# Weight low parts on one engine and four normalisations moved from VectorE to ScalarE, in a one-core layer tower

## The chip, the core and the metric

The kernel runs on one core of a Trainium2 chip. The metric is the device time of one execution in microseconds (us), as the median of several runs. Engines are named as in the profile: PE (TensorE matmul), PEld (its weight loads), DVE (VectorE), ACT (ScalarE), POOL (GpSimd) and SP (SyncE, which issues most DMAs).

## What is computed

Eight sequences of 512 tokens go through an embedding, a linear-attention block with memory, and a mixture of 64 experts with two shared ones, all in fp32. Cut to what matters here:

```python
h = concat(fine_embed[ids], softmax(cluster_logits[ids]) @ coarse_embed)   # (8, 512, 128)
x = layernorm(h)                                       # x1 in the kernel
xn = rms_norm(x)                                       # xn: one scale and shift of h
x = x + mem_scale * (((xn@q)(xn@k)^T * decay) @ (xn@v)) @ o
xn2 = rms_norm(x)
y = x + op_scale * gelu(xn2 @ read @ mix + bias) @ write
h = h + y
x3 = layernorm(h)
gates = top6(softmax(x3 @ router + bias)), with a capacity per expert
out = h + shared_ffn(x3) / 2 + sum_e gates[e] * (silu(x3@gate[e]) * (x3@up[e])) @ down[e]
```

## The kernel before

The experts are taken two at a time, as 33 **pairs** of 128 hidden columns (pair 0 is the shared one). For each pair `gate_up` (L470) issues three fp32r matmuls of 128x512 for gate and three for up, because each fp32 operand is held as a high part and a low part (`gate_hi`, `gate_lo`, `x_hi`, `x_lo`; the products are hi*hi, lo*hi and hi*lo). ACT applies Silu (L603), DVE multiplies by up (L855), POOL multiplies by the row of gates (L1016), and `down` (L449) adds the product into `bank_y`; for odd pairs `hid` is split too, by ACT (L609) and DVE (L861).

Each engine has its own instruction queue, written out by hand in one order. `sequences` (L259) calls one function per engine for each sequence b; its loop runs over p = 0..32, and at the slots of the tables `PE_AT`, `ACT_AT`, `DVE_AT`, `POOL_AT` it slips in the steps of the next sequence (`*_late(b+1)`, attention and router) and of the one after (`*_early(b+2)`, embedding). So the attention of sequence b+1 hides under the experts of sequence b. Sequence 0 has nothing to hide under: its early and late steps run alone, in an **opening** of two such loops ahead of `sequences` (pairs 0 and 1 of its experts are put there at slot 30). Banks: pair p of gate and of up uses one of two PSUM banks each, so `gate_up(p)` waits for Silu and the up product of pair p-2. `down` runs four pairs behind.

In the opening the weights arrive too: gate and up in six chunks of 11 pairs (`CHUNKS`, 704 KB each, issued by SP at L330), each into a staging buffer that is also something else (`hid`, `gate_rows`, `later`). `split_hi` (ACT, L637) copies the chunk rounded to fp32r into the high part; `split_lo` (L271, on DVE or on POOL by the table `LO_AT`) subtracts it to get the low part, and frees the buffer. Four staging buffers serve six chunks, so the last two chunks wait for a low part. `down_hi` (ACT, L656) and `down_lo` (DVE, L951) do the same for the down weights of odd pairs.

The four normalisations of a sequence, each four instructions of 128x128 on DVE, are `xn` (L671, slot 0), `x1` (L677, slot 5), `xn2` (L720, slot 11) and `x3` (L743, slot 19); the inverse roots come from POOL (L986, L992, L997). For example:

```python
last = dve.tensor_scalar(xn[:, t, :], emb[par][:, t, :], mv1[:, t, 0:1], inv1[:, 1, t:t + 1],
                         ALU.subtract, ALU.mult)
```

## Time and profile before

| | us |
|---|---|
| median of 3 runs (lowest, highest) | 746.45 (746.19, 747.09) |
| the profiled execution, its own time | 748.99 |
| its span, first to last instruction | 746.8 |
| busy in the span: PE, PEld | 689.9, 516.6 |
| busy in the span: DVE, POOL, ACT | 526.0, 471.0, 350.4 |

Busy time is the sum over an engine's instructions. A matmul's end is modelled and matmuls are pipelined, so PE's busy share tells only whether it had something in flight; how fast it went is seen from the distance between the starts of two matmuls, or from the granted clock. An instruction that is long because it was held up counts as busy for its whole length.

### The profile page before, as it was taken

The page shows a single profiled execution, that of the slowest core. Times are in us where ns is not written, and L with a number is a line of the kernel's source. Part 1 is how long each engine was busy: PE and PEld are TensorE (multiplying, and loading weights), DVE is VectorE, ACT ScalarE, POOL GpSimd, SP SyncE. Part 2 cuts the span into 40 slices and gives each one's busy share as a digit, 9 for nine tenths or more (in the row PEclk, how much of TensorE's full clock was granted, in tenths as well). Part 3 has the DMA queues.
Part 4 walks back from the last instruction along what each step waited for, and adds up shares of the span by engine and source line. Part 5 has one row for each costly group of instructions (what it writes and reads, how often), then busy time and mean ns, then how long its engine had stood idle before and what let it go on. Part 6 is the DMA issues. An engine that isn't in the chain of part 4 may idle for free.

```text
span 746.8 us, 10995 instructions
## 1 busy us (share of the span) xinstructions
PE 689.9 (92%) x2943; PEld 516.6 (69%) x2943; DVE 526.0 (70%) x1070; ACT 350.4 (47%) x607; POOL 471.0 (63%) x352
## 2 busy tenths in 40 slices
PE   4355799999999999989999999999999999999997
PEld 3244577777777767757777777777777777777775
DVE  4846767798678877775777886698777866684443
ACT  3323355534744455523645446544645445543342
POOL 5511657667676757656666766667766656676664
PEclk8555899999999999989999999999999999999999
DMA  5500423333333423333333333334334434335431
GB/s 206 205 1 0 121 85 106 107 110 112 110 100 113 119 88 116 111 99 109 95 107 112 109 111 110 113 82 133 107 100 114 120 93 119 100 112 136 131 123 57
DMA packets 48868, 80.31 MB, mean 108 GB/s; under 512 B 9504, under 2 KB 13728, under 8 KB 48800
## 3 DMA queue, kind: packets, MB, share of 16 engines
q1 hardware_dynamic: 47776, 77.44, 33.9%
q0 software_dynamic: 1024, 2.10, 1.3%
q8 instruction: 27, 0.44, 0.2%
q14 instruction: 41, 0.34, 0.1%
HBM read 76.35 MB, written 3.15 MB: 106 GB/s over the span
## 4 chain that ended last, share of the span: by engine, by line
PE 89%; DVE 5%; issue 2%; ACT 1%; POOL 0%; DVEq 0%; POOLq 0%
PE bank_y L468 15%; PE bank_g L479 8%; PE bank_g L480 8%; PE bank_u L481 8%; PE bank_u L479 8%; PE bank_g L481 8%; PE bank_u L480 8%; PE bank_y L463 4%; PE bank_y L462 4%; PE bank_y L465 4%; PE bank_f L387 1%; PE bank_f L409 1%; PE bank_f L403 1%; PE bank_f L420 1%; PE bank_f L379 1%
## 5 line engine op out<-in xcount | busy, mean ns | idle before, releaser
L1016 POOL TENSOR_TENSOR hid<-hid,gate_rows 128x512 f32<-128x512 f32 x256 | 372.5, 1464 | 195.9 <-DVE hid L855 193.2
L603 ACT ACTIVATE hid<-bank_g 128x512 f32<-128x512 f32 x264 | 156.6, 599 | 279.0 <-PE bank_g L481 268.2
L855 DVE TENSOR_TENSOR hid<-hid,bank_u 128x512 f32<-128x512 f32 x264 | 178.7, 681 | 139.5 <-PE bank_u L481 79.4
L479 PE MATMUL bank_g<-x_hi,gate_hi 128*128 128x512 f32 x264 | 144.1, 546 | 3.7 <-issue 3.7
L468 PE MATMUL bank_y<-hid,w_down 128*128 128x512 f32 x272 | 138.9, 592 | 0.0
L861 DVE TENSOR_TENSOR hid_lo<-hid,hid_hi 128x512 fp32r<-128x512 f32 x128 | 109.5, 855 | 2.6 <-issue 2.2
L480 PE MATMUL bank_g<-x_hi,gate_lo 128*128 128x512 f32 x264 | 105.5, 400 | 0.0
L481 PE MATMUL bank_u<-x_lo,up_hi 128*128 128x512 f32 x264 | 105.4, 399 | 0.0
L479 PE MATMUL bank_u<-x_hi,up_hi 128*128 128x512 f32 x264 | 105.3, 399 | 0.0
L481 PE MATMUL bank_g<-x_lo,gate_hi 128*128 128x512 f32 x264 | 105.2, 399 | 0.0
L480 PE MATMUL bank_u<-x_hi,up_lo 128*128 128x512 f32 x264 | 104.9, 397 | 0.0
L609 ACT ACTIVATE hid_hi<-hid 128x512 fp32r<-128x512 f32 x128 | 80.2, 627 | 7.9 <-POOL hid L1016 7.2
L479 PEld LDWEIGHTS bank_g<-x_hi,gate_hi 128*128 128x128 f32 x264 | 50.7, 192 | 28.9 <-issue 22.6
L480 PEld LDWEIGHTS bank_g<-x_hi,gate_lo 128*128 128x128 f32 x264 | 50.9, 193 | 23.7 <-issue 19.0
L468 PEld LDWEIGHTS bank_y<-hid,w_down 128*128 128x128 f32 x272 | 51.3, 189 | 11.9
L479 PEld LDWEIGHTS bank_u<-x_hi,up_hi 128*128 128x128 f32 x264 | 50.5, 191 | 12.1
L481 PEld LDWEIGHTS bank_g<-x_lo,gate_hi 128*128 128x128 f32 x264 | 50.3, 191 | 12.0
L481 PEld LDWEIGHTS bank_u<-x_lo,up_hi 128*128 128x128 f32 x264 | 50.1, 190 | 12.1
L480 PEld LDWEIGHTS bank_u<-x_hi,up_lo 128*128 128x128 f32 x264 | 50.2, 190 | 11.8
L462 PE MATMUL bank_y<-hid_hi,down_hi 128*128 128x512 f32 x128 | 52.0, 406 | 0.0
L463 PE MATMUL bank_y<-hid_hi,down_lo 128*128 128x512 f32 x128 | 51.5, 402 | 0.0
L465 PE MATMUL bank_y<-hid_lo,down_hi 128*128 128x512 f32 x128 | 51.1, 399 | 0.0
(197 smaller groups left out, 842.7 us busy)
## 6 DMA issues: line engine op xcount, KB each, us to landing
gate_rows<-gates_dram SPq DMA_DIRECT2D x512, 128.0 KB
hid<-gate_t_dram SPq DMA_DIRECT2D x3, 704.0 KB, 7.3
w_down<-down_t_dram SPq DMA_DIRECT2D x3, 704.0 KB, 6.7
out_dram<-later SPq DMA_DIRECT2D x8, 256.0 KB, 2.9
gate_rows<-up_t_dram SPq DMA_DIRECT2D x2, 704.0 KB, 4.9
gates_dram<-gates_t SPq DMA_DIRECT2D x8, 128.0 KB, 2.3
later<-up_t_dram SPq DMA_DIRECT2D x1, 704.0 KB, 8.5
shared<-square_w_dram SPq DMA_DIRECT2D x1, 512.0 KB
```

What stands on the lines that cost most here:

```text
L462: pe.matmul(y, down_hi[:, j, :], hid_hi[:, k, :], start=False, stop=False)
L463: pe.matmul(y, down_lo[:, j, :], hid_hi[:, k, :], start=False, stop=False)
L465: pe.matmul(y, down_hi[:, j, :], hid_lo[:, k, :], start=False, stop=False).then_inc(sem("down_done"), 1)
L468: pe.matmul(y, w_down[:, p, :], hid[:, slot(par, p), :], start=(p == 0), stop=(p == PAIRS - 1)).then_inc(sem("down_done"), 1)
L479: pe.matmul(o, w_hi[name][:, p, :], x3_hi[par][:, :], start=True, stop=False)
L480: pe.matmul(o, w_lo[name][:, p, :], x3_hi[par][:, :], start=False, stop=False)
L481: pe.matmul(o, w_hi[name][:, p, :], x3_lo[par][:, :], start=False, stop=True).then_inc(sem("pe_" + name), 1)
L603: act.activation(hid[:, slot(par, p), :], bank_g[(p + par) % 2][:, :], ACT.Silu).then_inc(sem("silu"), 1)
L609: act.activation(hid_hi[:, (p // 2) % SPLIT_RING, :], hid[:, slot(par, p), :], ACT.Copy)\
L855: dve.tensor_tensor(hid[:, s, :], hid[:, s, :], bank_u[(p + par) % 2][:, :], ALU.mult)\
L861: dve.tensor_tensor(hid_lo[:, k, :], hid[:, slot(par, p), :], hid_hi[:, k, :].bitcast(F32), ALU.subtract)\
L1016: pool.tensor_tensor(hid[:, s, :], hid[:, s, :], gate_rows[:, row, :], ALU.mult)\
```

## The change

The table `CHUNKS` now says of each chunk its staging buffer, the slot of its high part (ACT) and the slot of its low part, all on DVE (slots from 33 on lie in sequence 0's experts). The last two chunks have staging buffers of their own, so no chunk waits for another. `down_hi` goes from slot 26 to 10 of the opening, `down_lo` from slot 28 of the opening to slot 1 of sequence 0. DVE computes only the small shifts `-mean * inv` (`shift1`, `shift3`), and ACT does the normalisations as `Identity(scale * in + bias)`, `xn2` as a `Copy` with scale: `xn` in slot 0, `x1` in slot 3, `xn2` in slot 11, `x3` in slot 19. PE waits for the low parts chunk by chunk.

```diff
...
 SPLITS = PAIRS // 2
-DOWN_HI_AT, DOWN_LO_AT = 26, 28
+DOWN_HI_AT, DOWN_LO_AT = 10, PAIRS + 1
...
 GATHER_AT = (1, 2, 3, 4)
-DVE_AT = dict(xn=0, xn_lo=2, x1=5, xn_dec=5, y_lo=4, scores=6, state=6, x2=8, result=10, logits=9, xn2=11, exp_sum=12,
-              h=15, bn1=16, h2=17, bn3=17, mv1=18, x3=19, x3_lo=21, router=24, prob=26, top=27, chosen=28, gates=29,
+DVE_AT = dict(shift1=0, xn_lo=2, xn_dec=5, y_lo=4, scores=6, state=6, x2=8, result=10, logits=9, exp_sum=12,
+              h=15, bn1=16, h2=17, bn3=17, mv1=18, shift3=19, x3_lo=21, router=24, prob=26, top=27, chosen=28, gates=29,
               taken=31)
...
              router=23, gates_t=30)
-ACT_AT = dict(xn_hi=2, y_hi=4, z=6, ffn_t=5, squares=9, squares2=10, cluster_exp=10, exp_t=12, xn2_t=13, vals=14,
+ACT_AT = dict(xn=0, x1=3, xn2=11, x3=19, xn_hi=2, y_hi=4, z=6, ffn_t=5, squares=9, squares2=10, cluster_exp=10, exp_t=12, xn2_t=13, vals=14,
               x3_hi=21, router_exp=24)
...
 CHUNK = 11
-CHUNKS = [(n, p0) for p0 in range(0, PAIRS, CHUNK) for n in ("gate", "up")]
-HI_AT = (-20, -20, -20, -20, 4, 5)
-LO_AT = (("pool", -10), ("vector", 0), ("pool", -10), ("vector", 0), ("pool", 0), ("vector", 6))
-RAW_PARTS = 4
+CHUNKS = (("gate", 0, "hid0", None, -20, 3),
+          ("up", 0, "rows", None, -20, 10),
+          ("gate", CHUNK, "hid1", None, 3, 14),
+          ("up", CHUNK, "later", None, 5, 14),
+          ("gate", 2 * CHUNK, "own0", None, 5, PAIRS + 6),
+          ("up", 2 * CHUNK, "own1", None, 7, PAIRS + 9))
+CHUNK_OF = {(n, p0): k for k, (n, p0, *_) in enumerate(CHUNKS)}
 SHIFT = 3
...
         inv1 = sb("inv1", [P, 2, TILES])
+        shift1 = sb("shift1", [P, 2, TILES])
+        shift3 = sb("shift3", [P, TILES])
         x1 = sb("x1", [P, TILES, D])
...
-        raw = [b.rearrange("p r s -> p (r s)")[:, 0:CHUNK * P].rearrange("p (c d) -> p c d", c=CHUNK)
-               for b in (hid[:, 0:RING // 2, :], gate_rows[:, :, :], hid[:, RING // 2:RING, :], later[:, :, :])]
+        def staging(b):
+            return b.rearrange("p r s -> p (r s)")[:, 0:CHUNK * P].rearrange("p (c d) -> p c d", c=CHUNK)
+        raw = {"hid0": staging(hid[:, 0:RING // 2, :]), "hid1": staging(hid[:, RING // 2:RING, :]),
+               "rows": staging(gate_rows[:, :, :]), "later": staging(later[:, :, :]),
+               "own0": sb("raw0", [P, CHUNK, P])[:, :, :], "own1": sb("raw1", [P, CHUNK, P])[:, :, :]}
         gates_dram = nc.dram_tensor("gates_dram", (BATCHES, EXPERTS, SEQ), F32, kind="Internal").ap()
...
-        def weights_split(eng, chunks):
+        def staging_free(eng, buffer):
-            for part in range(min(RAW_PARTS, chunks)):
-                eng.wait_ge(sem(f"split_lo{part}"), (chunks - 1 - part) // RAW_PARTS + 1)
+            for k, c in enumerate(CHUNKS):
+                if c[2] == buffer:
+                    eng.wait_ge(sem(f"split_lo{k}"), 1)
-        def split_lo(eng, name, at):
-            for k, (n, p0) in enumerate(CHUNKS):
-                if LO_AT[k] == (name, at):
-                    eng.wait_ge(sem("split_hi"), k + 1)
-                    eng.tensor_tensor(w_lo[n][:, p0:p0 + CHUNK, :], raw[k % RAW_PARTS],
+        def split_lo(dve, at):
+            for k, (n, p0, buffer, _, _, lo_at) in enumerate(CHUNKS):
+                if lo_at == at:
+                    dve.wait_ge(sem(f"split_hi{k}"), 1)
+                    dve.tensor_tensor(w_lo[n][:, p0:p0 + CHUNK, :], raw[buffer],
                                       w_hi[n][:, p0:p0 + CHUNK, :].bitcast(F32), ALU.subtract)\
-                       .then_inc(sem(f"split_lo{k % RAW_PARTS}"), 1)
+                       .then_inc(sem(f"split_lo{k}"), 1)
+            if at == DOWN_LO_AT:
+                dve.wait_ge(sem("down_hi"), 1)
+                dve.tensor_tensor(down_lo[:, :, :], odd_pairs(w_down), down_hi[:, :, :].bitcast(F32), ALU.subtract)\
+                   .then_inc(sem("down_lo"), 1)
...
                 if isinstance(b, int) and b == 0:
-                    weights_split(sp, len(CHUNKS))
+                    staging_free(sp, "rows")
             if r >= GATE_RING:
...
-            def weights(k):
-                n, p0 = CHUNKS[k]
-                part = k % RAW_PARTS
-                if k >= RAW_PARTS:
-                    sp.wait_ge(sem(f"split_lo{part}"), k // RAW_PARTS)
-                sp.dma_start(raw[part], sources[n][:, p0:p0 + CHUNK, :]).then_inc(sem(f"raw{part}"), 16)
             sp.wait_ge(sem("gathered0"), 16 * TILES)
-            for k in range(len(CHUNKS)):
-                weights(k)
+            for k, (n, p0, buffer, before, _, _) in enumerate(CHUNKS):
+                if before is not None:
+                    sp.wait_ge(sem(f"split_lo{before}"), 1)
+                sp.dma_start(raw[buffer], sources[n][:, p0:p0 + CHUNK, :]).then_inc(sem(f"raw{k}"), 16)
             for p0 in range(0, PAIRS, CHUNK):
...
             q = PAIRS * b + p
+            if isinstance(b, int) and b == 0 and p % CHUNK == 0:
+                for n in ("gate", "up"):
+                    pe.wait_ge(sem(f"split_lo{CHUNK_OF[n, p]}"), 1)
             ring = (p + par) % 2
...
                     pe.wait_ge(sem("x3_lo"), 1)
-                    weights_split(pe, 2 * PAIRS // CHUNK)
                     for k in range(AHEAD):
...
             f0, f1 = bank_f
+            for name, k, out in (("xn", 1, xn), ("x1", 0, x1)):
+                if p == ACT_AT[name]:
+                    act.wait_ge(sem("shift1"), b + 1)
+                    for t in range(TILES):
+                        last = act.activation(out[:, t, :], emb[par][:, t, :], ACT.Identity,
+                                              scale=inv1[:, k, t:t + 1], bias=shift1[:, k, t:t + 1])
+                    last.then_inc(sem(name), 1)
+            if p == ACT_AT["xn2"]:
+                act.wait_ge(sem("inv2"), b + 1)
+                act.wait_ge(sem("xn_dec"), b + 1)
+                for t in range(TILES):
+                    last = act.activation(xn2[:, t, :], x2[:, t, :], ACT.Copy, scale=inv2[:, t:t + 1])
+                last.then_inc(sem("xn2"), 1)
+            if p == ACT_AT["x3"]:
+                act.wait_ge(sem("shift3"), b + 1)
+                for t in range(TILES):
+                    last = act.activation(x3[:, t, :], h2[par][:, t, :], ACT.Identity,
+                                          scale=inv3[:, t:t + 1], bias=shift3[:, t:t + 1])
+                last.then_inc(sem("x3"), 1)
             if p == ACT_AT["xn_hi"]:
...
             act.wait_ge(sem("pe_gate"), q + 1)
-            if isinstance(b, int) and b == 0 and p == 0:
-                weights_split(act, len(CHUNKS))
+            if isinstance(b, int) and b == 0 and p in (0, RING // 2):
+                staging_free(act, "hid1" if p else "hid0")
             wait(act, "down_done", q - RING + 1)
...
                     act_early(act, b + 2, p)
+                if first:
+                    split_hi(act, PAIRS + p)
                 act_silu(act, b, par, p)
...
         def split_hi(act, at):
-            for k, (n, p0) in enumerate(CHUNKS):
-                if HI_AT[k] == at:
-                    part = k % RAW_PARTS
-                    act.wait_ge(sem(f"raw{part}"), 16 * (k // RAW_PARTS + 1))
-                    act.activation(w_hi[n][:, p0:p0 + CHUNK, :], raw[part], ACT.Copy).then_inc(sem("split_hi"), 1)
+            for k, (n, p0, buffer, _, hi_at, _) in enumerate(CHUNKS):
+                if hi_at == at:
+                    act.wait_ge(sem(f"raw{k}"), 16)
+                    act.activation(w_hi[n][:, p0:p0 + CHUNK, :], raw[buffer], ACT.Copy).then_inc(sem(f"split_hi{k}"), 1)
...
             f0, f1 = bank_f
-            if p == DVE_AT["xn"]:
+            if p == DVE_AT["shift1"]:
                 dve.wait_ge(sem("inv1"), b + 1)
-                for t in range(TILES):
-                    last = dve.tensor_scalar(xn[:, t, :], emb[par][:, t, :], mv1[:, t, 0:1], inv1[:, 1, t:t + 1],
-                                             ALU.subtract, ALU.mult)
-                last.then_inc(sem("xn"), 1)
-            if p == DVE_AT["x1"]:
-                for t in range(TILES):
-                    last = dve.tensor_scalar(x1[:, t, :], emb[par][:, t, :], mv1[:, t, 0:1], inv1[:, 0, t:t + 1],
-                                             ALU.subtract, ALU.mult)
-                last.then_inc(sem("x1"), 1)
+                dve.scalar_tensor_tensor(shift1[:, :, :], mv1[:, :, 0].unsqueeze(1).to_broadcast([P, 2, TILES]), -1.0,
+                                         inv1[:, :, :], ALU.mult, ALU.mult).then_inc(sem("shift1"), 1)
             if p == DVE_AT["xn_dec"]:
...
                    .then_inc(sem("x2"), 1)
-            if p == DVE_AT["xn2"]:
-                dve.wait_ge(sem("inv2"), b + 1)
-                for t in range(TILES):
-                    last = dve.tensor_scalar(xn2[:, t, :], x2[:, t, :], inv2[:, t:t + 1], None, ALU.mult)
-                last.then_inc(sem("xn2"), 1)
             if p == DVE_AT["h2"]:
...
                 dve.tensor_scalar(var3[:, :], mv3[:, :, 1], LN_EPS, None, ALU.add).then_inc(sem("var3"), 1)
-            if p == DVE_AT["x3"]:
+            if p == DVE_AT["shift3"]:
                 dve.wait_ge(sem("inv3"), b + 1)
-                for t in range(TILES):
-                    last = dve.tensor_scalar(x3[:, t, :], h2[par][:, t, :], mv3[:, t, 0:1], inv3[:, t:t + 1],
-                                             ALU.subtract, ALU.mult)
-                last.then_inc(sem("x3"), 1)
+                dve.scalar_tensor_tensor(shift3[:, :], mv3[:, :, 0], -1.0, inv3[:, :], ALU.mult, ALU.mult)\
+                   .then_inc(sem("shift3"), 1)
             if p == DVE_AT["x3_lo"]:
...
                     dve_early(dve, b + 2, par, p, use)
+                if first:
+                    split_lo(dve, PAIRS + p)
                 dve_up(dve, b, par, p)
...
                         .then_inc(sem("decays"), 1)
-                split_lo(dve, "vector", p - PAIRS)
             dve.wait_ge(sem("decays"), 3)
...
                 dve_early(dve, 1, 1, p - SHIFT, 1, bank_y)
-                split_lo(dve, "vector", p)
-                if p == DOWN_LO_AT:
-                    dve.wait_ge(sem("down_hi"), 1)
-                    dve.tensor_tensor(down_lo[:, :, :], odd_pairs(w_down), down_hi[:, :, :].bitcast(F32), ALU.subtract)\
-                       .then_inc(sem("down_lo"), 1)
+                split_lo(dve, p)
             sequences(dve, lambda *a: dve_sequence(dve, *a))
...
                 pool_early(pool, 0, p)
-                split_lo(pool, "pool", p - PAIRS)
             for p in range(PAIRS):
...
                 pool_early(pool, 1, p - SHIFT)
-                split_lo(pool, "pool", p)
             sequences(pool, lambda *a: pool_sequence(pool, *a))
...
```

ACT's queue in the opening, from the second high part on: before,

```order
L637 ACTIVATE up_hi<-gate_rows 128x1408
L637 ACTIVATE gate_hi<-hid 128x1408
L637 ACTIVATE up_hi<-later 128x1408
L560 ACTIVATE x_hi<-bank_f 128x512
L563 ACTIVATE vo_y_hi<-bank_f 128x512
L637 ACTIVATE gate_hi<-hid 128x1408
L637 ACTIVATE up_hi<-gate_rows 128x1408
L567 ACTIVATE z<-bank_f 128x256 x2
L573 ACTIVATE shared,ss<-shared 128x128 x4
L577 ACTIVATE xn_t<-bank_f 128x512
```

and with the change:

```order
L664 ACTIVATE up_hi<-gate_rows 128x1408
L570 ACTIVATE xn<-emb,shift,inv 128x128 x4
L587 ACTIVATE x_hi<-bank_f 128x512
L570 ACTIVATE x<-emb,shift,inv 128x128 x4
L664 ACTIVATE gate_hi<-hid 128x1408
L590 ACTIVATE vo_y_hi<-bank_f 128x512
L664 ACTIVATE up_hi<-later 128x1408
L664 ACTIVATE gate_hi<-raw 128x1408
L594 ACTIVATE z<-bank_f 128x256 x2
L664 ACTIVATE up_hi<-raw 128x1408
L600 ACTIVATE shared,ss<-shared 128x128 x4
L683 ACTIVATE down_hi<-w_down 128x2048
```

`x<-` is `x1`, `shared,ss` the squares for `xn2`. The normalisations stand between the high parts; `x1` and one high part now lie ahead of `vo_y_hi`.

ACT's queue where sequence 0's experts begin, before,

```order
L587 ACTIVATE turns<-turns 128x256
L656 ACTIVATE down_hi<-w_down 128x2048
L603 ACT_TABLE_LOAD
L603 ACTIVATE hid<-bank_g 128x512 x2
L560 ACTIVATE x_hi<-bank_f 128x512
```

and with the change:

```order
L614 ACTIVATE turns<-turns 128x256
L570 ACTIVATE xn<-emb,shift,inv 128x128 x4
L630 ACT_TABLE_LOAD
L630 ACTIVATE hid<-bank_g 128x512 x2
L587 ACTIVATE x_hi<-bank_f 128x512
```

`hid<-bank_g` is Silu. The normalisation for sequence 1 now stands ahead of the table load and of the first two Silus. All over the program ACT has 33 rows with a table load before and 33 after.

DVE's queue where sequence 0's experts begin, up to the state of the attention, before,

```order
L807 SCALAR_TENSOR_TENSOR gates_t<-taken,bank_f 64x512
L671 TENSOR_SCALAR xn<-emb,mv,inv 128x128 x4
L855 TENSOR_TENSOR hid<-hid,bank_u 128x512 x2
L686 TENSOR_TENSOR x_lo<-bank_f,x_hi 128x512
```

and with the change:

```order
L817 SCALAR_TENSOR_TENSOR gates_t<-taken,bank_f 64x512
L696 SCALAR_TENSOR_TENSOR shift<-mv,inv 128x8
L865 TENSOR_TENSOR hid<-hid,bank_u 128x512
L287 TENSOR_TENSOR down_lo<-w_down,down_hi 128x2048
L865 TENSOR_TENSOR hid<-hid,bank_u 128x512
L704 TENSOR_TENSOR x_lo<-bank_f,x_hi 128x512
```

`hid<-hid,bank_u` is the up product. `down_lo` came ahead of the gates before, and now lies between the first two up products; a `gate_lo` and an `up_lo` of 128x1408 follow in slots 6 and 9.

## Rows read from the trace of the kernel before

**Rows 1.** Busy by stage: PE, PEld, DVE, ACT, POOL, clock, DMA share, GB/s.
```profile
22.00:75.00 53.00, 26.88 (x93) 20.48 (x93) 33.87 (x83) 16.08 (x27) 11.53 (x8) 0.56 0.19 68
...
100.00:180.00 80.00, 78.95 (x341) 58.59 (x341) 60.97 (x123) 41.95 (x73) 54.88 (x41) 1.00 0.35 107
```

**Rows 2.** Chain that ended last, 0:105: start, us, what.
```profile
19.16 3.00 DVE decay_cols L941
...
22.19 3.91 DVE xn L671 x4
26.10 3.07 DVE up_lo L271 x2
29.17 0.61 DVE x_lo L686
...
45.36 1.29 ACT shared L573 x8
```

**Rows 3.** Line L271, the low parts, by engine.
```profile
L271 POOL TENSOR_TENSOR gate_lo<-hid,gate_hi x3: 3144/3156/3193, 19.0 to 33.5; 128x1408 fp32r<-128x1408 f32 x3
L271 DVE TENSOR_TENSOR up_lo<-gate_rows,up_hi x2: 1611/1614/1618, 26.0 to 41.0; 128x1408 fp32r<-128x1408 f32 x2
```

**Rows 4.** Timeline of the opening: start, us, engine, line, what, count.
```profile
18.27 0.15 DVE L932 TENSOR_TENSOR mem_mul<-rows 128x1 f32<-128x1 f32 x1
...
27.37 0.60 ACT L560 ACTIVATE x_hi<-bank_f 128x512 fp32r<-128x512 f32 x1 [5.97 <-PE bank_f L352]
...
31.57 0.60 ACT L563 ACTIVATE vo_y_hi<-bank_f 128x512 fp32r<-128x512 f32 x1 [3.61 <-PE bank_f L360]
32.07 1.37 ACT L637 ACTIVATE gate_hi<-hid 128x1408 fp32r<-128x1408 f32 x1
...
33.27 4.03 DVE L677 TENSOR_SCALAR x<-emb,mv,inv 128x128 f32<-128x128 f32 x4
...
36.44 0.66 ACT L567 ACTIVATE z<-bank_f 128x256 f32<-128x256 f32 x2 [1.74 <-PE bank_f L371]
...
48.17 1.86 DVE L720 TENSOR_SCALAR xn<-shared,inv 128x128 f32<-128x128 f32 x4 [2.85 <-POOL inv L986]
```

**Rows 5.** Groups of ACT, by form: busy, mean ns, idle before.
```profile
L573 ACT ACTIVATE shared<-shared 128x128 f32<-128x128 f32 x32 | 9.5, 299 | 8.3 <-DVE shared L715 8.3
...
L580 ACT ACTIVATE vals<-bank_f,cols 128x512 f32<-128x512 f32 x8 | 5.5, 689 | 0.6 <-PE bank_f L403 0.6
...
L577 ACT ACTIVATE xn_t<-bank_f 128x512 f32<-128x512 f32 x8 | 4.8, 599 | 14.4 <-PE bank_f L397 14.4
```

**Rows 6.** Timeline, opening's end and sequence 0.
```profile
60.39 1.11 DVE L743 TENSOR_SCALAR xn<-h,mv,inv 128x128 f32<-128x128 f32 x4 [0.80 <-POOL inv L992]
...
67.06 1.90 ACT L656 ACTIVATE down_hi<-w_down 128x2048 fp32r<-128x2048 f32 x1
...
68.97 1.28 ACT L603 ACT_TABLE_LOAD   x1
...
70.57 2.26 DVE L951 TENSOR_TENSOR down_lo<-w_down,down_hi 128x2048 fp32r<-128x2048 f32 x1
...
78.62 0.78 PE L479 MATMUL bank_g<-x_hi,gate_hi 128*128 128x512 f32 x1
```

**Rows 7.** Timeline, pair 8 of sequence 0 ends.
```profile
101.66 1.02 PE L468 MATMUL bank_y<-hid,w_down 128*128 128x512 f32 x2
```

**Rows 8.** Timeline, pairs 2 to 8 of sequence 1, first and last.
```profile
165.10 0.47 PE L479 MATMUL bank_g<-x_hi,gate_hi 128*128 128x512 f32 x1
...
185.22 1.02 PE L468 MATMUL bank_y<-hid,w_down 128*128 128x512 f32 x2
```

**Rows 9.** What PE waited for, 100:747: us in total, times, longest.
```profile
PE bank_f L379 <- issue: 3.8, 4, 1.2
PE bank_g L479 <- issue: 3.7, 1, 3.7
```

**Rows 10.** Timeline of DVE in sequence 1.
```profile
173.91 3.23 DVE L677 TENSOR_SCALAR x<-emb,mv,inv 128x128 f32<-128x128 f32 x4
```

## The prediction

> **What bounds the kernel now.** I read the busy time by stage first. From 100 us on the kernel is bound by PE: in 100:180 PE has something in flight for 78.95 of 80 us at full clock, DVE is busy for 60.97, POOL for 54.88, ACT for 41.95; the later stages look the same. The opening is another matter: in 22:75 PE is busy for 26.88 of 53 us at a clock of 0.56 [rows 1]. There one engine waits for the next, so every instruction on the chain counts in full. What the change can win lies in the first 100 us and in the few waits of PE after it.
>
> The chain of the opening shows where. DVE's `decay_cols`, one column wide, takes 3.00 us, `xn` 3.91 us, and then two low parts of the weights stand ahead of `x_lo`, which starts at 29.17 [rows 2]. The reason is in the groups of L271: a low part takes 3.16 us on POOL and 1.61 on DVE, and POOL's first starts at 19.0 [rows 3], together with `decay_cols`. `decay_cols` lasts as long as POOL's first, and `xn` as long as the second and 0.8 us more: while POOL works on SBUF, these instructions of DVE don't go on.
>
> **The opening, step by step.** Gains are negative; the sum is what a point of the program moves by.
>
> 1. Without POOL's low parts `decay_cols` should cost 0.15, as its one-column neighbour `mem_mul` does [rows 4], and end at 19.3 in place of 22.16. `shift1` is put at 0.2 us. Then ACT runs `xn`. What does ACT take? A 128x128 activation lasts 299 ns; a bias read per partition makes 689 of 599 at 128x512, so 90 ns more [rows 5]. Scale by a pointer is not in the trace: between 0 and 90 ns. I take 90, the nearest row, so 479 ns each; two following ones overlap by 0.1 us (`vo_y_hi` ends at 32.17, the next began at 32.07 [rows 4]), and four take 1.62 us (1.26 if the scale is free). `xn` ends at 21.15 in place of 26.10. After `xn` the transposes and `x_hi` take 1.87 (26.10 to 27.97, where `x_hi` ends [rows 4]) and now `x_lo` follows at once: it starts at 23.0, not at 29.17. **-6.1.**
> 2. `x1` and a high part of 1.37 us [rows 4] are now ahead of `vo_y_hi` on ACT: 22.95 + 1.62 + 1.37 less overlaps is 25.75, where its input is ready at 25.45. **+0.3** (to -5.8; `vo_y_hi` starts at 25.75, not 31.57 [rows 4]).
> 3. `x1` on DVE went from 33.27 to 37.30, beyond the end of ACT's `z` at 37.10 [rows 4], with `decay` and scores behind it. Taken away, the scores wait for `z` alone. **-0.85** (to -6.65).
> 4. `xn2`. The squares end at 46.64 [rows 2], DVE starts at 48.17 and needs 1.86 [rows 4], so 3.4 us in all. Now `down_hi`, 1.90 [rows 6], goes behind the squares, and hides the root on POOL; then four activations with one pointer, 1.26: 3.1 us. **-0.3** (to -6.95).
> 5. `x3`: four on DVE take 1.11 [rows 6]; `shift3` and four on ACT take 0.2 and 1.62. **+0.7** (to -6.25).
> 6. `down_lo`, 2.26 us on DVE ahead of the gates [rows 6], of which 2.1 are on the chain, goes. **-2.1** (to -8.35).
> 7. `xn` of sequence 1 on ACT with its shift takes 1.85 in place of 1.1. **+0.75** (to -7.6). And here something turns: ACT's load of the Silu table, 1.28 us, ran at 68.97, long before it was needed [rows 6]. Now it and Silu (0.6) stand behind `xn`. `gate_up(2)` waits for that Silu: it starts 1.9 us after `xn` and not 0.75 after it, when the transposes are issued. **+1.15** (to -6.45). `gate_up(2)` starts at 72.15, not at 78.62 [rows 6].
>
> A page speaks against steps 5 and 7. The Trainium skill (ScalarE: Activation LUTs, "Rules for kernel authors") wants add and multiply on VectorE, not on ScalarE. By that the trace agrees for one instruction alone; by step 4 it doesn't where DVE is held up by POOL. The same page ("What ACT_TABLE_LOAD costs") gives 93 ns to each pointer operand; by it `xn` takes the 1.62 above.
>
> The other four high parts lie in gaps of ACT. The low parts in slots 3, 10 and 14 lie in DVE's waits: there PE and ACT work on the memory, `xn2_t` and `vals`, which take longer than 2 x 1.61. The DMAs of the last two chunks have no wait any more and `w_down` lands earlier; nothing waited for them before, so I cost that at nothing. If chunk two or three were late, ACT would stand still ahead of `vo_y_hi`, which is why I leave 1 us for it in the range.
>
> **Sequence 0.** Pairs 2 to 8 took from 78.62 to 101.66 [rows 6, 7], 23.0 us. The same seven pairs in sequence 1 took from 165.10 to 185.22 [rows 8], 20.1 us, with one wait of PE of about 1.05 in them (3.8 in four [rows 9] makes 0.95 on average) and two `down` that sequence 0 doesn't have, 1.5 together (one of fp32 is 1.02 long [rows 8], the three matmuls of an odd pair less): 17.5. The half clock at the start adds about 1.6 in both versions, an estimate: eight matmuls at double distance. So at most 23.0 - 19.1 = 3.9 can be won. Before, DVE was late there (`x1` alone held it for 3.23 in sequence 1 [rows 10]); this goes to ACT. But `down_lo` (2.26) and `gate_lo` (1.61) come in. Walking both queues forward, DVE is in time for the first and late by 0 to 1 us for the second. I take **-3.5** (bounds -1 and -3.9; to -9.95). Then `up_lo` in slot 9, with POOL at work beside it, is 1.6 to 3.1 us; PE waits between 0 and 3 us. **+1** (to -8.95).
>
> **Sequences 1 to 7.** PE waited 3.8 us in four places for L379, the state [rows 9]. In each DVE was late with the scores because `x1` stood ahead of them: 3.23 us [rows 10]. With `x1` on ACT in slot 3, where ACT waits for PE anyway, DVE reaches the scores by the time `z` is there. **-3.5** of the 3.8 (to -12.45). The hole of 3.7 us at `gate_up` [rows 9] has no releaser ("issue"), all engines stand still in it, and it lies at the backward jump of the loop: it stays. What gives nothing: DVE is relieved of all four normalisations, but it isn't the bound. ACT gets 3 x 1.62 + 1.26 = 6.1 us more per sequence on 42 of 80: it holds. In slot 0 ACT now waits for DVE, and Silu 0 comes 2.1 us later; `gate_up(2)`, which needs it, comes a pair later, and a pair takes 20.1 / 7 = 2.9 us. In slot 19 and in slot 11 the delay is under 1.3 us against the same two pairs.
>
> **Sum.** 748.99 - 12.45 = 736.5 for the profiled execution. That execution lies 2.54 above the median of 746.45, so I forecast 734.0. A difference under 0.2%, 1.5 us, can't be told from no change here.
>
> **Rivals.**
> - *Sequence 0 chokes on the low parts.* DVE's big subtractions and POOL's products exclude each other; each costs 3.1 us and not 1.6, PE runs dry in slots 9 to 11 and its clock falls to half again, as in the opening, 0.56 [rows 1]. For it: the 3.00 us of `decay_cols` [rows 2]. By the Trainium skill (SBUF — State Buffer, "SBUF: two separate sides") VectorE and GpSimd lock a shared port pair for a whole instruction each, against this move of the work to the time when POOL is busiest; the trace agrees in `decay_cols`. Against the rival: DVE gives off `x1` and `xn2` there. Steps -3.5 and +1 become -1 and +3, and 1 us of clock: 734.0 + 5.5 = 739.5.
> - *Everything is hidden.* The scale pointer is free (three chains of four, -1.1), PE runs the seven pairs at once (-0.4), `up_lo` costs nothing (-1), and all of the 3.8 is won (-0.3): 731.2. If the hole at the jump closes too, another -3.7 [rows 9], but nothing in the change speaks for that.
> - *ACT becomes the bound (the other side).* The place is Silu: its queue now holds two sets that wait for DVE and two that are long. If the room of two pairs is not there, each of six sequences pays its 6.1 us of normalisations: +37, so 771. It decides if ACT's wait in slot 0 grows beyond some 3 us; it takes 2 us per sequence to eat the whole gain. The rule of the Trainium skill named above (ScalarE: Activation LUTs) would have this one. Against: 42 us of 80 [rows 1].
> - *The change doesn't do what it says:* `Identity` may not be in the table that is loaded. Two loads of 1.28 at each of 24 places would make +61 on ACT, half of it hidden: 765. The number of load rows is the same, so this is nearly excluded.
>
> **How the numbers follow.** Forecast 0.58, choked sequence 0 0.20, everything hidden 0.15, ACT the bound 0.04, no proper table 0.01, and 0.02 for no change at all, if the opening's slack goes to a wait that I don't see. The range takes the first three with the bounds of `xn` and of the chunks: 728.5 to 740, of the hole's 3.7 the most part left out. Faster by over 0.2%: 0.93; within it: 0.02; slower: 0.05.
>
> **What would show it.** In the new profile: `decay_cols` under 0.3 us and `x_lo` near 23; ACT's four `xn` in 1.6 us; squares to the end of `xn2` in 3.1; `gate_up(2)` near 72; the table load right behind `xn`; pair 8 done near 92; no wait at the state in sequences 1 to 6; the hole at the loop still there. I am wrong if Silu waits on ACT's own queue in the steady part, if DVE's low parts in slots 6 and 9 show waits of PE above 3 us, or if the gain of the opening is under 5 us.

## The result, and the profile after

The forecast was wrong in size and in sign.

| | before | after |
|---|---|---|
| median of 7 runs each (lowest, highest), us | 746.19 (744.60, 747.19) | 751.04 (749.16, 752.68) |
| ratio, 95% interval | | 1.0068 (1.0049 to 1.0088) |
| the profiled execution, its own time; span | 748.99; 746.8 | 749.28; 747.5 |
| busy: DVE, POOL, ACT | 526.0, 471.0, 350.4 | 497.1, 461.0, 394.4 |

734.0 was forecast, 728.5 to 740.0 as the range. The two profiled executions lie 2.8 above and 1.8 below their medians; the comparison of traces below is made on them, so it has to explain 0.7 us of span, while the medians are 4.85 apart. The other 4 us lie in executions of which there is no trace; where they arise is not shown.

**The opening came as forecast.** The timeline of after (start, us, engine, line, what):

```profile
19.51 0.16 DVE L953 TENSOR_TENSOR decay_cols<-decay_out,decay_full 128x1 f32<-128x1 f32 x1
...
19.91 1.65 ACT L570 ACTIVATE xn<-emb,shift,inv 128x128 f32<-128x128 f32 x4 [2.60 <-DVE shift L696]
...
23.45 0.69 DVE L704 TENSOR_TENSOR x_lo<-bank_f,x_hi 128x512 fp32r<-128x512 f32 x1 [3.58 <-ACT x_hi L587]
...
26.12 0.58 ACT L590 ACTIVATE vo_y_hi<-bank_f 128x512 fp32r<-128x512 f32 x1
...
70.34 1.28 ACT L630 ACT_TABLE_LOAD   x1
...
72.29 0.79 PE L488 MATMUL bank_g<-x_hi,gate_hi 128*128 128x512 f32 x1 [0.79 <-ACT hid L630]
```

`decay_cols` fell from 3.00 us [rows 2] to 0.16, `x_lo` starts at 23.45 (23.0 said, 29.17 before), and `gate_up(2)`, which waits for a Silu behind the exposed table load, starts at 72.29, where 72.15 was said and 78.62 was before [rows 6]. In the chain of after:

```profile
40.60 1.80 ACT down_hi L683
42.40 1.22 ACT xn L577 x4
...
54.16 1.66 ACT xn L582 x4
```

**The price of an activation was right too.** Groups of ACT by form in after (busy, mean ns, idle before): two pointers make 483, one makes 390, where none made 299 [rows 5].

```profile
L570 ACT ACTIVATE xn<-emb,shift,inv 128x128 f32<-128x128 f32 x32 | 13.2, 483 | 25.3 <-DVE shift L696 25.3
...
L577 ACT ACTIVATE xn<-shared,inv 128x128 f32<-128x128 f32 x32 | 10.2, 390 | 3.2 <-POOL inv L993 3.2
...
L582 ACT ACTIVATE xn<-h,shift,inv 128x128 f32<-128x128 f32 x16 | 6.6, 482 | 16.2 <-DVE shift L754 16.2
```

**Then the gain is given back, sequence by sequence.** I took the start of every `gate_up` in both traces. After minus before is -6.33 at pair 2 of sequence 0, -6.52 at pair 8 (the -3.5 of pairs 2 to 8 did not come), -5.64 at the start of sequence 1, and +0.69 at the start of sequence 7. An undisturbed sequence (sequence 1, start to start) takes 84.01 us before and 85.83 after. The 1.8 us lie in three places: +0.76 at pair 6, +0.43 at pair 20, +0.45 at pairs 25 and 26; what is left is small change. The waits of after in 85:747 (engine, line, waited for: us, times, longest) name pair 6:

```profile
DVE hid L865 <- ACT hid L630: 91.9, 47, 2.8
...
ACT xn L582 <- DVE shift L754: 25.7, 7, 3.7
...
ACT xn L570 <- DVE shift L696: 15.5, 6, 4.1
...
PE bank_f L385 <- issue: 10.8, 6, 2.1
```

The state step (L385, L379 before) now costs PE 1.8 to 2.1 us in five of its six places. The one of sequence 0 (2.1) cost 2.0 before as well; from 100 us on it cost 1.2 at most [rows 9], and sequence 3, at the loop's jump, had no such wait at all. DVE waits for ACT's Silu in 47 places; before it was 58.5 us in 24.

Why? Sequence 1 of after, slots 0 to 6. `x<-` is `x1`, `shared<-bank_f` are the scores:

```profile
155.50 0.66 DVE L696 SCALAR_TENSOR_TENSOR shift<-mv,inv 128x8 f32<-128x8 f32 x1
156.20 1.65 ACT L570 ACTIVATE xn<-emb,shift,inv 128x128 f32<-128x128 f32 x4 [2.21 <-DVE shift L696]
...
158.36 0.69 DVE L865 TENSOR_TENSOR hid<-hid,bank_u 128x512 f32<-128x512 f32 x1 [2.20 <-ACT hid L630]
...
159.25 1.76 POOL L1027 TENSOR_SCALAR hid<-hid 128x512 f32<-128x512 f32 x1 [1.87 <-DVE hid L865]
...
165.09 2.32 DVE L871 TENSOR_TENSOR hid_lo<-hid,hid_hi 128x512 fp32r<-128x512 f32 x1 [1.08 <-ACT hid_hi L636]
...
170.35 3.50 DVE L871 TENSOR_TENSOR hid_lo<-hid,hid_hi 128x512 fp32r<-128x512 f32 x1
...
170.78 2.52 POOL L1023 TENSOR_TENSOR hid<-hid,gate_rows 128x512 f32<-128x512 f32 x2
173.78 0.74 DVE L717 TENSOR_TENSOR shared<-bank_f,decay_mask 128x256 f32<-128x256 f32 x2
174.62 0.91 PE L385 MATMUL bank_f<-z,shared 128*128 128x128 f32 x6 [1.81 <-issue]
```

and the same place before:

```profile
163.26 0.68 DVE L855 TENSOR_TENSOR hid<-hid,bank_u 128x512 f32<-128x512 f32 x1
...
164.14 1.76 POOL L1020 TENSOR_SCALAR hid<-hid 128x512 f32<-128x512 f32 x1 [1.40 <-DVE hid L855]
...
177.98 0.68 DVE L861 TENSOR_TENSOR hid_lo<-hid,hid_hi 128x512 fp32r<-128x512 f32 x1
178.21 1.57 POOL L1016 TENSOR_TENSOR hid<-hid,gate_rows 128x512 f32<-128x512 f32 x1 [1.18 <-DVE hid L855]
178.58 0.74 DVE L699 TENSOR_TENSOR shared<-bank_f,decay_mask 128x256 f32<-128x256 f32 x2
179.42 0.91 PE L379 MATMUL bank_f<-z,shared 128*128 128x128 f32 x6 [1.05 <-issue]
```

Sequence 1 begins at 159.98 before and at 154.34 after; from there the product of pair 0 on DVE comes at 3.28 and at 4.02, POOL's scaling of it at 4.16 and 4.91, the scores at 18.60 and 19.44. So the state is late by what POOL is late by. And `hid_lo` of pair 3, 0.68 long before, now lasts 3.50: it starts just ahead of two products of POOL and ends 0.55 us behind the second, about the time it takes when it is free. `x1` had filled that very time: it was held for its 3.23 us [rows 10] and kept `hid` from DVE's queue, so POOL paused and `hid_lo` fell into the pause.

### The profile page after: what moved, and what is told of

The parts are those of the page before. It is cut to its first block, busy times and chain, and to the rows that moved or that the text cites. A ratio compares the mean times of both kernels' runs of the same rounds, so it can differ in the third digit from the quotient of the medians.

```text
span 747.5 us, 11019 instructions
## 1 busy us (share of the span) xinstructions
PE 693.6 (93%) x2943; PEld 512.0 (68%) x2943; DVE 497.1 (67%) x961; ACT 394.4 (53%) x735; POOL 461.0 (62%) x349
## 4 chain that ended last, share of the span: by engine, by line
PE 60%; issue 14%; POOL 11%; DVE 6%; ACT 4%; DMA 1%; SPq 0%; POOLq 0%; ACTq 0%; DVEq 0%
PE bank_y L474 11%; POOL hid L1023 9%; PE bank_g L488 6%; PE bank_u L488 5%; PE bank_u L490 5%; PE bank_u L489 5%; PE bank_g L489 5%; PE bank_g L490 5%; PE bank_y L471 3%; PE bank_y L469 2%; PE bank_y L468 2%; DVE hid_lo L871 1%; PE bank_f L393 1%; PE bank_f L385 1%; POOL inv L999 1%
## 5 line engine op out<-in xcount | busy, mean ns | idle before, releaser
L1023 POOL TENSOR_TENSOR hid<-hid,gate_rows 128x512 f32<-128x512 f32 x256 | 368.7, 1451 | 203.4 <-DVE hid L865 201.2
L871 DVE TENSOR_TENSOR hid_lo<-hid,hid_hi 128x512 fp32r<-128x512 f32 x128 | 133.4, 1042 | 9.8 <-ACT hid_hi L636 9.8
L490 PEld LDWEIGHTS bank_g<-x_lo,gate_hi 128*128 128x128 f32 x264 | 50.1, 190 | 11.8
```

Of the source, the lines that this page charges most:

```text
L490: pe.matmul(o, w_hi[name][:, p, :], x3_lo[par][:, :], start=False, stop=True).then_inc(sem("pe_" + name), 1)
L871: dve.tensor_tensor(hid_lo[:, k, :], hid[:, slot(par, p), :], hid_hi[:, k, :].bitcast(F32), ALU.subtract)\
L1023: pool.tensor_tensor(hid[:, s, :], hid[:, s, :], gate_rows[:, row, :], ALU.mult)\
```

## The experiments

Twelve kernels, timed in five rounds each. They ran in three groups, each with the kernel before beside it (747.79, 747.54 and 747.36). After was timed only beside the 746.19 of the first table, so a difference between an experiment and its 751.04 carries 1.2 to 1.6 us of what the kernel before moved between the groups; the ratios don't. Theory A, made from the trace of after: VectorE, freed of `x1`, comes early and is held by POOL in `hid_lo(3)`. The last columns are read in the traces: the start of `gate_up(2)` in the opening, and one undisturbed sequence. The first of these moves by itself: e1 and e7 have the same opening and are 0.96 us apart, after and e5 0.08.

| run | what is different | median, us | ratio to before | `gate_up(2)` | sequence 1 |
|---|---|---|---|---|---|
| before | | | | 78.62 | 84.01 |
| after | | 751.04 | 1.0068 (1.0049, 1.0088) | 72.29 | 85.83 |
| e1_plan_only | new plan, normalisations on DVE | 739.21 | 0.9879 (0.9852, 0.9906) | 68.72 | 84.04 |
| e2_norms_only | old plan, normalisations on ACT | 758.39 | 1.0130 (1.0102, 1.0159) | 79.19 | 85.78 |
| e3_x3_back | after, `x3` on DVE | 740.77 | 0.9913 (0.9884, 0.9941) | 70.16 | 84.59 |
| e4_x1_back | after, `x1` on DVE | 750.64 | 1.0038 (1.0022, 1.0054) | 71.10 | 85.78 |
| e5_scores_first | after, `hid_lo(3)` behind the scores | 737.01 | 0.9851 (0.9826, 0.9877) | 72.21 | 83.79 |
| e6_before_scores_first | the same in the kernel before | 743.17 | 0.9951 (0.9934, 0.9968) | 78.65 | 83.39 |
| e7_best | e1 with the scores first | 733.54 | 0.9816 (0.9797, 0.9835) | 67.76 | 83.50 |
| e8_x3_back_scores_first | e3 and e5 together | 730.13 | 0.9773 (0.9755, 0.9791) | 69.87 | 82.91 |
| e9_xn_back | after, `xn` on DVE | 746.54 | 0.9988 (0.9973, 1.0004) | 69.61 | 85.59 |
| e10_xn_x3_back | after, `xn` and `x3` on DVE | 736.58 | 0.9865 (0.9841, 0.9889) | 68.09 | 84.41 |
| e11_shift1_early | after, `shift1` in slot 22 | 741.20 | 0.9917 (0.9895, 0.9940) | 68.71 | 84.14 |
| e12_three_edits | e8 and e11 together | 725.98 | 0.9716 (0.9693, 0.9738) | 67.44 | 82.91 |

**The two halves of the change.** In e1 the normalisations are back on DVE in their old slots; e2 has their move alone, over the old plan:

```diff
-DVE_AT = dict(shift1=0, xn_lo=2, ...
+DVE_AT = dict(xn2=11, x1=5, shift1=0, xn_lo=2, ...
...
-ACT_AT = dict(xn=0, x1=3, xn2=11, x3=19, xn_hi=2, ...
+ACT_AT = dict(xn=0, x1=3, xn2=-99, x3=-99, xn_hi=2, ...
...
-            for name, k, out in (("xn", 1, xn), ("x1", 0, x1)):
+            for name, k, out in ():
```

are lines of e1 against after. The four loops of DVE are back in `dve_late`, `xn` and `x3` in the places of the two shifts (slots 0 and 19). e2 against before has

```diff
-ACT_AT = dict(xn_hi=2, ...
+ACT_AT = dict(xn=0, x1=3, xn2=11, x3=19, xn_hi=2, ...
```

with the shifts and ACT's four loops as in after.

> The new plan of the weights' low parts, with the four normalisations left on VectorE in their old slots. Theory A (the plan wins in the opening, ScalarE's normalisations lose some 1.8 us in each of six sequences): no loss per sequence against before, the opening better by the 6.3 us of the changed kernel and by 3 more (no table load behind xn, four on VectorE 1.1 us and not 1.66), so 746.2 - 9 = 737, between 734 and 740. Theory B (the big subtractions on VectorE in sequence 0, or the later start of the steady part, are what costs): no better than 748. Theory C (the difference comes from the hole at the loop's jump alone, which has a length of its own in each execution): between 744 and 751 whatever the parts.

> The old plan of the low parts (two engines, four staging buffers), with the four normalisations on ScalarE. Theory A: six sequences lose 1.8 us each (+11), the opening wins 1 to 3 because xn isn't held up by GpSimd's low part but loses the table load; together 752 to 758. Theory B: about as before, 744 to 748. Theory C: 744 to 751.

The plan alone wins 8.6 us, the normalisations alone lose 10.6 (0.4 more than the range allowed). All of the loss per sequence is theirs: 85.78 in e2 is the 85.83 of after. In the opening, too, the credit that step 1 gave to ScalarE belongs to the plan: `gate_up(2)` comes at 68.72 with DVE normalising and no low part on POOL, 3.6 us sooner than in after (0.6 of it because TensorE's eight matmuls of L415 took 1.45 us there and 2.08 in after), and not sooner at all (79.19, before 78.62) with ACT normalising over the old plan.

**Which normalisation, and which wait.** e3, `x3` alone back:

```diff
             if p == DVE_AT["shift3"]:
                 dve.wait_ge(sem("inv3"), b + 1)
-                dve.scalar_tensor_tensor(shift3[:, :], mv3[:, :, 0], -1.0, inv3[:, :], ALU.mult, ALU.mult)\
-                   .then_inc(sem("shift3"), 1)
+                for t in range(TILES):
+                    last = dve.tensor_scalar(x3[:, t, :], h2[par][:, t, :], mv3[:, t, 0:1], inv3[:, t:t + 1],
+                                             ALU.subtract, ALU.mult)
+                last.then_inc(sem("x3"), 1)
```

> The changed kernel with x3 alone back on VectorE. Theory A: TensorE's extra 0.43 us ahead of the transposes of x3 and the 0.45 us at pairs 25 to 27 (Silu behind a router step that is late by as much as x3) both go, in seven sequences, and 0.7 in the opening: -6, so 745. If the 0.45 at pairs 25 to 27 has another cause: -3.5, so 747.5. Theory B or C: 750 to 751.

It won 10.3 us (751.04 to 740.77), more than expected. The losses at pairs 20, 25 and 26 go, as said, but 0.36 of the 0.76 at pair 6 of the next sequence goes with them, and 2.1 us in the opening, of which only 0.7 is `x3`'s step. The other 1.4 were there before `x3` began, and they are TensorE's pace. The same six matmuls of the state, first in after and then in e3:

```profile
32.31 1.62 PE L385 MATMUL bank_f<-z,shared 128*128 128x128 f32 x6 [1.38 <-ACT z L594]
```

```profile
32.32 0.91 PE L385 MATMUL bank_f<-z,shared 128*128 128x128 f32 x6 [1.38 <-ACT z L594]
```

They give 0.7 us, the matmuls behind them 0.3 and L415 0.4. The edit touches none of this, and e4 and e12 show pieces of the same in their openings, so this part is luck of the execution. Slot 19 of sequence 1 in after shows how:

```profile
208.00 1.02 POOL L999 TENSOR_TENSOR inv<-var,neg_half 128x4 f32<-128x4 f32 x1
209.00 1.28 POOL L1023 TENSOR_TENSOR hid<-hid,gate_rows 128x512 f32<-128x512 f32 x1
...
209.05 1.25 DVE L754 SCALAR_TENSOR_TENSOR shift<-mv,inv 128x4 f32<-128x4 f32 x1 [0.32 <-POOL inv L999]
...
210.34 1.65 ACT L582 ACTIVATE xn<-h,shift,inv 128x128 f32<-128x128 f32 x4 [3.71 <-DVE shift L754]
```

`shift3`, 512 numbers, takes 0.16 in the opening and 1.25 here: it starts with a product of POOL and ends with it. ACT stands for 3.71 us with two Silu behind it, then works for 1.65. `x3` is ready 2.94 us after its shift could start; DVE took 2.08 for it at the same place of before, and the 0.86 between them matches the +0.88 of pairs 20, 25 and 26. How much of that is the held shift and how much the activations was not run: no experiment computes `shift3` early or unheld.

e5 moves `hid_lo` of pair 3 behind the scores of slot 6:

```diff
+LO_HELD = 5
...
                 last.then_inc(sem("scores"), 1)
+                if held is not None:
+                    dve_lo(dve, *held)
...
-                if p >= SPLIT_LAG and is_split(p - SPLIT_LAG):
+                if p == LO_HELD and late:
+                    pass
+                elif p >= SPLIT_LAG and is_split(p - SPLIT_LAG):
                     dve_lo(dve, b, par, p - SPLIT_LAG)
```

> The changed kernel with one instruction moved: VectorE's hid_lo of pair 3 goes behind the scores of slot 6. In the changed kernel this hid_lo takes 3.5 us because it meets two products of GpSimd on SBUF, and the scores and TensorE's state wait behind it. Theory A: TensorE's wait at the state (1.9 us in five places) goes, -9, so 742. A rival, that the scores are late through ScalarE's z or through the up product: the wait stays at 1.5 or more and the time at 750.

737.01, a gain of 14 us where 9 were expected; 11.8 of it are in the traces, 1.8 in sequence 0, 2.0 to 2.3 in each of sequences 1 to 4 and 1.4 in sequence 5. Its timeline in sequence 1:

```profile
169.24 0.75 DVE L718 TENSOR_TENSOR shared<-bank_f,decay_mask 128x256 f32<-128x256 f32 x2 [0.69 <-ACT z L595]
169.91 2.06 DVE L874 TENSOR_TENSOR hid_lo<-hid,hid_hi 128x512 fp32r<-128x512 f32 x1
...
170.81 0.83 PE L386 MATMUL bank_f<-z,shared 128*128 128x128 f32 x6
```

The scores now wait for `z` (ACT), and PE for nothing. `hid_lo` is still held (2.06, 0.68 when free), but nothing waits for it. This fits A; it does not show who makes it late.

e4 and e6 ask that. e6 is e5's edit over the kernel before; e4 puts `x1` back in its old slot:

```diff
-DVE_AT = dict(shift1=0, ...
+DVE_AT = dict(x1=5, shift1=0, ...
...
-            for name, k, out in (("xn", 1, xn), ("x1", 0, x1)):
+            for name, k, out in (("xn", 1, xn),):
...
+            if p == DVE_AT["x1"]:
+                for t in range(TILES):
+                    last = dve.tensor_scalar(x1[:, t, :], emb[par][:, t, :], mv1[:, t, 0:1], inv1[:, 0, t:t + 1],
+                                             ALU.subtract, ALU.mult)
+                last.then_inc(sem("x1"), 1)
```

> The changed kernel with the four tiles of x1 alone back on VectorE in slot 5. Theory A (VectorE, freed of x1, comes to the low part of hid(3) and to the scores at a time when GpSimd's gated products hold their lock, so that TensorE waits longer at the state step): the growth of that wait, 0.75 us a sequence in six places, goes away and nothing else does, the losses at pairs 20 and 25 stay: 746.5, between 745 and 748. Theory B (the wait at the state step grew for another reason, the later x3 or the new plan, and x1 is not its cause): within 1 us of the changed kernel, 750 to 752, with the wait at pair 6 unchanged, or longer by x1's own 0.85 us a sequence where VectorE's queue sets the scores: up to 755.

> The kernel before with one edit: VectorE's low part of hid(3) stands behind the scores of slot 6 instead of ahead of them. Theory A (the wait for the state step, 1.05 to 1.17 us in sequences 1 to 3 of the trace of before, is what hid_lo ahead of the scores costs): minus 1.1 to 1.4 us a sequence in 4 or 5 places, 741 to 743 against 747.8. Rival (the low part is then late for its down product and that wait takes its place): no change, 747 to 749.

e6 gains 4.4 us (0.2 less than its range wanted): the wait that the kernel before had is the same one. e4 overthrows A. With `x1` back on DVE the median is within 1 us of after's (0.3% lower by the ratios), and the sequence stays as it was, 85.78 with +0.67 at pair 6 in place of +0.76:

```profile
169.28 3.23 DVE L700 TENSOR_SCALAR x<-emb,mv,inv 128x128 f32<-128x128 f32 x4
...
173.35 0.68 DVE L876 TENSOR_TENSOR hid_lo<-hid,hid_hi 128x512 fp32r<-128x512 f32 x1
173.96 0.74 DVE L722 TENSOR_TENSOR shared<-bank_f,decay_mask 128x256 f32<-128x256 f32 x2
...
174.80 0.91 PE L385 MATMUL bank_f<-z,shared 128*128 128x128 f32 x6 [1.72 <-DVE shared L722]
```

`hid_lo` is short again, and `x1` is long, held by POOL in its turn. The scores come 19.36 us into the sequence, in after 19.44: with `x1` or without it, DVE is through there when POOL's products let it be. So the question is what makes POOL late. (In the expectations that follow, what is called Silu(1) and hid(1) is the pair 0, and hid_hi(4) and hid_lo(4) are those of pair 3.)

> The changed kernel with xn alone back on VectorE (x1, xn2 and x3 stay on ScalarE). Theory C, which takes the place of A after x1 was moved back alone and changed nothing: the delay at the state step is handed on in a queue. Silu(1) stands on ScalarE behind xn, which stands behind shift1; it comes 2.0 us late, so that VectorE's hid(1) and then GpSimd's products come 0.75 us late, and with them hid_hi(4), hid_lo(4) and the scores. Of the 0.75 us, 0.36 come from x3 (router late) and 0.40 from xn in slot 0. C expects at pair 6 a loss against the kernel before of 0.36 in place of 0.75 us, six times, so 748.6, between 747 and 750. Rival D (the delay is the sum of small things, any one of which is absorbed): no change at pair 6, 750 to 752.

> The changed kernel with xn and x3 back on VectorE, so that x1 and xn2 alone are on ScalarE. Theory C: the whole 0.75 us at pair 6 and the 0.88 us at pairs 20 to 26 are gone, and x1 and xn2 on ScalarE neither gain nor lose: within 1.5 us of the kernel with the plan alone, so 738 to 740.5. Theory A as it stood before (x1 off VectorE brings the low part of hid(3) into GpSimd's products, the scores come later for it): 0.8 us a sequence more than that, 742 to 745. The forecast on record (x1 off VectorE ends the state wait): 734.

> The changed kernel with shift1 computed in slot 22 of the sequence before, as soon as GpSimd has inv1, and not in slot 0; all four normalisations stay on ScalarE. It tells whether the loss through xn comes from ScalarE's wait for VectorE (2.2 us ahead of xn in slot 0) or from the 1.65 us of xn themselves. Theory C1 (the wait): ScalarE does xn while it would wait for gate 1 anyway, the loss at pair 6 falls from 0.75 to about 0.36; and in the opening xn and the Silu table load of sequence 1 run before the gates, gate_up(2) comes 2 to 4 us sooner: 745.5, between 743 and 748. Theory C2 (the activations themselves): pair 6 keeps its 0.75, only the opening gains: 747 to 749.

e9 puts `xn` back, e10 `xn` and `x3`, and e11 moves `shift1`:

```diff
-            for name, k, out in (("xn", 1, xn), ("x1", 0, x1)):
+            for name, k, out in (("x1", 0, x1),):
...
+                for t in range(TILES):
+                    last = dve.tensor_scalar(xn[:, t, :], emb[par][:, t, :], mv1[:, t, 0:1], inv1[:, 1, t:t + 1],
+                                             ALU.subtract, ALU.mult)
+                last.then_inc(sem("xn"), 1)
```

is e9's, behind the line of `shift1`, and e11's is

```diff
-DVE_AT = dict(shift1=0, ...
+DVE_AT = dict(shift1=22, ...
```

with the four lines of `shift1` moved from `dve_late` to `dve_early`, so that ACT finds it ready.

None of the three landed in its range: 746.54, 736.58 and 741.20 are 0.5, 1.4 and 1.8 us under C's.

e9: pair 6 gives back 0.2, not the 0.4 of theory C, for the four `xn` on DVE are themselves held (2.16 us), and `hid` of pair 0 stands behind them. The median is 4.5 lower; in the traces sequence 7 starts 2.4 sooner, of which 1.9 were there at the start of sequence 1.

e10: 84.41 a sequence against 84.04 of e1, so `x1` and `xn2` on ACT win nothing there; the rest, 0.35 at pair 6, I put to `shift1` (0.65 us), which still stands on DVE ahead of `xn`, without a run of its own. Its median is 2.6 below e1's, of which 4 us are the stretch at the loop's jump (last section) and 0.7 the opening. The forecast's 734 and A's 742 to 745 are both out.

e11 decides for pair 6: all four normalisations stay on ACT, with all their time, and the loss there goes from +0.76 to -0.93, further than C1 said. Sequence 1 of e11:

```profile
151.63 1.64 ACT L570 ACTIVATE xn<-emb,shift,inv 128x128 f32<-128x128 f32 x4
...
154.17 0.69 DVE L866 TENSOR_TENSOR hid<-hid,bank_u 128x512 f32<-128x512 f32 x1 [0.86 <-ACT hid L630]
...
155.11 1.93 POOL L1028 TENSOR_SCALAR hid<-hid 128x512 f32<-128x512 f32 x1
...
166.89 3.03 DVE L872 TENSOR_TENSOR hid_lo<-hid,hid_hi 128x512 fp32r<-128x512 f32 x1
...
169.84 0.74 DVE L713 TENSOR_TENSOR shared<-bank_f,decay_mask 128x256 f32<-128x256 f32 x2
```

The sequence begins at 152.09: POOL's scaling comes at 3.0 (4.9 in after), the scores at 17.75 (19.44). At pair 6 it was ACT's wait for a 0.66 us instruction of DVE, not the activations. The loss at pairs 20, 25 and 26, behind `shift3`, stays in e11 (+0.85).

**The pieces together.** e7, e8 and e12 join edits shown above.

> The new plan for the weights' low parts, all four normalisations on VectorE in their old slots, and the low part of hid(3) behind the scores. Theory A (the two gains are independent: the plan gives 8.6 us as its own run showed, the reordered scores 1.1 to 1.4 us in five or six places): 732.5, between 731 and 735. Rival (with the normalisations on VectorE the low parts that now stand behind the scores are late, or VectorE's x2 step is): 737 to 740.

> The changed kernel with two edits: x3 back on VectorE, and the low part of hid(3) behind the scores. Theory A (three losses, each in its own place: 0.43 us at pair 20 and 0.45 at pairs 25 and 26 belong to x3 on ScalarE, the state wait to the low part ahead of the scores): 737.0 of the run with the scores first, less 0.88 us in six sequences: 731.8, between 730 and 734, the fastest of all, since xn and x1 are off VectorE and x3 and the scores are not late. Rival (x3 on ScalarE costs nothing once the state wait is gone, the gain of taking x3 back having come through the state wait): 736 to 738.

> The changed kernel with three edits: x3 back on VectorE, the low part of hid(3) behind the scores, and shift1 computed in slot 22 of the sequence before. With the state wait gone already (the run with the first two edits shows none), the early shift can win only in the opening: 730.1 less 2 to 4, so 727, between 726 and 730. Rival: nothing more to win, because the first gated product waits for the gates and not for Silu: 729 to 731.

All three came within 2 us. e8 beats e7 by 3.4; 2.0 of that are the stretch at the loop's jump (last section), but 0.6 a sequence, all at pair 6, are not: with the two waits gone `xn`, `x1` and `xn2` on ACT are worth something after all, 82.91 a sequence against 83.50. In e12 PE waits after 100 us for one thing, once:

```profile
PE bank_f L498 <- ACT later L642: 0.7, 1, 0.7
```

e12 at 725.98 (724.99 to 726.57) beats both kernels: 2.8% under before, and by the two ratios 3.5% under after. Of the 23.7 us between the traces of before and e12, 5.0 are the stretch at the jump.

## Why the prediction was wrong

- *The opening, -6.45:* right, -6.33, and most of the steps to 0.5 us. Its reason was half right: e1 shows that the plan does it all, and that `gate_up(2)` comes 3.6 sooner without the normalisations on ACT (3.0 of it, net, steps 5 and 7 and, unforeseen, `xn` in step 1: once POOL is quiet DVE does it in 1.12 us, ACT in 1.65). And with TensorE's pace of e3 it would have been some 1.4 more, so that the size was met to 0.1 is in part luck.
- *Sequence 0, -3.5:* wrong. From the start of pair 2 to that of pair 8 it took 21.37 us in place of 21.56. The two large parts of this -0.19 are TensorE's clock: pair 3 took 1.14 more, since the granted clock was 0.50 up to 78 us, 5.7 us behind `gate_up(2)` (before up to 82, 3.3 behind it), and pair 7 took 1.55 less, since it was 1.00 in 96:99 where before had 0.51. The prediction had put the half clock at the same 1.6 in both. PE's wait at the state stayed (2.1 us, 2.0 before): DVE was not slow by its own work but held by POOL, and giving off `x1` frees it of nothing. The +1 for the rest of the sequence was right in size (+0.88), but 0.8 of it stands at pairs 20, 25 and 26 and is `x3`'s, not `up_lo`'s.
- *Sequences 1 to 7, "-3.5 of the 3.8":* this is the step that failed. From 100 us on PE's waits at the state were to fall from 3.8 us to 0.3 and rose to 8.8. I read `x1`'s 3.23 us as its cost; it was POOL's. What stands in that place instead, `hid_lo(3)`, takes 3.50. And with "Silu 0 comes 2.1 us later; `gate_up(2)`, which needs it, comes a pair later" I had the right delay (2.0) and asked one consumer only, PE. The other is DVE's product of pair 0, behind it POOL's queue, and that clocks the state. +0.71 to +0.76 in each of four sequences, and +2.3 in sequence 3, where before had no wait.
- *"In slot 19 and in slot 11 the delay is under 1.3 us":* slot 11 yes (Silu 1.2 late); in slot 19 ACT waits for 3.7, Silu comes 3.6 late, and +0.88 a sequence follows. I had priced `shift3` by what it does, not by what POOL does beside it. The Trainium skill (SBUF — State Buffer, "SBUF: two separate sides") says that VectorE and GpSimd lock a shared port pair for a whole instruction each; the trace agrees down to the smallest: 0.16 free, 1.25 beside a product. I had brought that rule against the low parts and not against the shifts.
- *ACT becomes the bound (0.04):* its place, Silu behind `xn` and `x3`, and its threshold, 2 us per sequence, were right (1.8 measured); its cause was not. In 100:180 ACT was busy for 44.29 of 80 us, DVE for 58.49:

```profile
100.00:180.00 80.00, 78.02 (x343) 57.60 (x342) 58.49 (x111) 44.29 (x80) 55.40 (x42) 1.00 0.33 103
```

An engine need not be full to cost time; it is enough that it waits with something behind it. 0.05 for slower was far too little for a change that puts two new waits across engines on a queue.
- *The hole stays, 0:* it did not stay put, nor did all engines stand still in it: DVE began `xn` at 331.37 before, 1.0 us ahead of PE. The stretch round the loop's jump (pair 31 of sequence 2 to pair 11 of sequence 3, less the same stretch of the sequences before) costs 5.0 us before and 1.75 after, which hides 3.3 of the 9.6 us that the sequences lost, and is one reason why the profiled executions are only 0.7 apart.

Counted in the traces: -6.33 - 0.19 + 0.88 + 9.6 - 3.3 = +0.7.

## What to carry to other kernels

Before moving work to a less busy engine, list what is queued behind it there and follow every consumer, not only the bound engine. A busy time longer than the operation's own size explains is somebody else's time, and moving the instruction away leaves it for the next one. Feed the moved work from something that is ready long before (e11), or reorder so that what is held is what nobody waits for (e5): the change of 0.7% for the worse became 2.8% for the better by three edits, the two named here and `x3` taken back, none of which removes work (0.7 of the 2.8% is the stretch at the jump).
